# Token attention, mixer and expert layer on one core: folded value-output weight, column-tiled gate and router, eight Gelu buffers, three conv sets

## The chip, the core and the metric

The kernel runs on one core of a Trainium2 chip. The metric is the device time of one execution in microseconds (us); lower is better. A core has a matrix engine (PE, with its weight loads PEld), a vector engine (DVE), a scalar engine for table functions (ACT), a general engine (POOL) and a sync engine (SP) that issues most DMAs. Each runs its own list of instructions in order, and they meet at semaphores only.

## The reference

All arithmetic is fp32. There are 16 images of 96 x 96 and 16 texts of 128 tokens of width 64.

```python
feat = conv2x2_stride2(x) + conv_b                  # 4 channels -> 144 tokens of 64
Q, K, V = feat @ wq.T + bq, feat @ wk.T + bk, feat @ wv.T + bv
tok = softmax(Q @ K.T / 8) @ V @ wo.T + bo
h = concat([tok, txt])                              # 272 tokens for each image
x = layernorm(h)
pos  = running sums of (x@Wvp+bvp) * cos/sin(base_phases), read out, / sqrt(position)
cont = running sums over key phases tanh(tanh(x@Wk1)@Wk2)*pi, read by query phases
gates = softmax(relu(x @ Wg1 + bg1) @ Wg2 + bg2)    # 2 numbers for each token
h = h + (layernorm(gates0*pos + gates1*cont) * ln_g + ln_b) @ Wo + bo
y = layernorm(h)
w = softmax over the two best of y @ Wg + bg        # 8 experts
out = h + sum_e w[e] * (gelu(y @ W1[e] + b1[e]) @ W2[e] + b2[e])   # 64 -> 256 -> 64
```

## The kernel before

Two images form a pair: one lies in partitions 0 to 63, the other in 64 to 127, so there are 8 pairs of 272 columns, 2176 columns in all, or 17 windows of 128 columns. Token attention and the mixer's phases, memory and recall run pair by pair. Layer norms, gate, routing and experts run by 5 groups of windows, `GW = [3, 4, 4, 4, 2]`. A norm needs the features of a token side by side, so a group is transposed by PE before it (h0_t, combine) and back after it (xn_t, norm_s, xn2_t).

The order of work on each engine is written out by hand in `PLAN`: a list of stages with an index for "pe", "dve", "act", "pool" and "sp". Each engine's block loops over its list and issues the instructions of the stage, with the semaphore waits that it needs. `BANKS` names the PSUM bank for each stage and index; `take` in the PE block makes a stage wait until the last reader of its bank is done.

The stages, with their lines:

- **Start.** SP loads the pixels in two halves (`pixa`, `pixb`), weights and text; ACT's queue loads phase, cols, ident, rows (L469 to L472). PE runs ten warm-up matmuls (L865). ACT makes the first tap of the convolution for each half (L478), DVE adds the other three (L618), the first half at once, the second as stages taps:0 to taps:2.
- **Token attention**, by pair: qkv (PE L873 to L877, evicted by DVE L682 and ACT L494, L498), scores (L888), row maximum (DVE L695), Exp with its sums (ACT L504), normalising (DVE L702), transposes (L898) copied by ACT (L514), mix (L909), evicted by ACT with the value bias (L520), tok_out (L915), evicted by ACT into `h0s` (L524).
- **base** (once): DVE reduces the base phases (L671 to L676), ACT takes the sines (L485 to L488), POOL scales them.
- **Mixer**: norm (moments L637 to L649, root on POOL L428, normalise L656), mix_gate (L943: stationary 128 tokens, moving the 32 columns of `g1_w`), gate_z on DVE (L718 to L723: bias, relu times weight difference, sum, bias), Tanh (L538); values (L963) and running sums (L746, L750); hidden and phases (L954, L982), absolute pass on DVE (L756), Sin (L554), memory (L993), mask (L766), recall (L1004, copied by L558); content (L970, L736); combine (L1017, L774 to L778), norm, attn_out (L1030).
- **Routing**, by group: route (L1038: stationary 128 tokens, moving the 16 columns of `gate_w`), the two best of 8 with their one-hots on DVE (L803 to L810), Tanh (L568), weights (L815 to L822), transposed (L1044), written to DRAM and read back broadcast over 64 partitions (`wide`) by SP.
- **Experts**, by group and expert: `expert` (L1070) makes two halves j of the hidden layer, each into two banks by two row tiles; ACT's Gelu (L592) writes one of four buffers `hidden_e`; `expert_out` (L1083) makes the output in two column tiles; DVE adds bias and weights it (L841); POOL adds it up (L463). `finish` (L1055) transposes the sum back, DVE adds it to `res` (L847), SP stores.

ACT's functions come from tables; a change of table shows as ACT_TABLE_LOAD.

## Time and profile before

| | us |
|---|---|
| median of 3 runs | 257.95 |
| all runs | 256.1, 263.72, 257.95 |
| profiled execution: span from first to last instruction | 254.6 |
| PE, DVE, ACT, POOL busy in it | 232.3, 170.6, 158.7, 100.7 |

The profile is of one execution; of its own time the page gives the span. Busy is the time in which an engine has an instruction running; matmuls are pipelined and their ends are modelled, so neighbouring matmuls overlap in it, and starts are the better measure of pace. Windows give busy time by engine in a stretch, with the number of instructions, TensorE's granted clock (1.00 is 2.4 GHz) and the DMA share. Every matmul of the code stands twice in the trace, as two instructions.

### The profile page before, as it was taken

The page shows a single profiled execution, that of the slowest core. Times are in us where ns is not written, and L with a number is a line of the kernel's source. Part 1 is how long each engine was busy: PE and PEld are TensorE (multiplying, and loading weights), DVE is VectorE, ACT ScalarE, POOL GpSimd, SP SyncE. Part 2 cuts the span into 40 slices and gives each one's busy share as a digit, 9 for nine tenths or more (in the row PEclk, how much of TensorE's full clock was granted, in tenths as well). Part 3 has the DMA queues.
Part 4 walks back from the last instruction along what each step waited for, and adds up shares of the span by engine and source line. Part 5 has one row for each costly group of instructions (what it writes and reads, how often), then busy time and mean ns, then how long its engine had stood idle before and what let it go on. Part 6 is the DMA issues. An engine that isn't in the chain of part 4 may idle for free.

```text
span 254.6 us, 4573 instructions
## 1 busy us (share of the span) xinstructions
PE 232.3 (91%) x1511; PEld 128.0 (50%) x1511; DVE 170.6 (67%) x526; ACT 158.7 (62%) x295; POOL 100.7 (40%) x88
## 2 busy tenths in 40 slices
...
GB/s 224 172 225 4 1 3 0 0 3 0 3 3 0 3 0 3 5 173 76 0 0 9 190 140 4 0 0 23 236 111 0 0 28 239 113 0 3 161 48 62
DMA packets 12902, 14.41 MB, mean 57 GB/s; under 512 B 6448, under 2 KB 10576, under 8 KB 12752
## 3 DMA queue, kind: packets, MB, share of 16 engines
...
q8 instruction: 12, 0.20, 0.3%
q14 instruction: 10, 0.08, 0.1%
...
## 4 chain that ended last, share of the span: by engine, by line
PE 61%; DVE 21%; ACT 9%; issue 6%; DMA 1%; POOLq 0%; POOL 0%; DVEq 0%; ACTq 0%
PE ps L1070 24%; PE ps L1083 23%; ACT probs L504 3%; DVE trig L756 2%; DVE stat L637 2%; DVE feat L618 2%; DVE y L746 2%; PE ps L993 2%; PE ps L1030 2%; PE ps L1004 1%; DMA arena<-in_x_a 1%; DVE mem L766 1%; PE ps L1038 1%; DVE negmax L695 1%; PE ps L933 1%
## 5 line engine op out<-in xcount | busy, mean ns | idle before, releaser
L592 ACT ACTIVATE arena<-ps,cols 128x1024 f32<-128x1024 f32 (+2 forms) x80 | 74.0, 984 | 45.9 <-PE ps L1070 34.2
L1070 PE MATMUL ps<-xt,w 64*128 64x512 f32 (+2 forms) x320 | 69.2, 556 | 1.0 <-ACT arena L592 0.4
L1083 PE MATMUL ps<-arena,w 128*64 128x512 f32 (+2 forms) x320 | 64.9, 538 | 0.7 <-ACT arena L592 0.7
L463 POOL TENSOR_TENSOR acc<-acc,scaled 128x512 f32<-128x512 f32 (+2 forms) x35 | 39.6, 1131 | 63.9 <-DVE scaled L841 63.0
L428 POOL TENSOR_TENSOR rstd<-vare,minus_half 128x8 f32<-128x8 f32 (+2 forms) x15 | 25.6, 1710 | 65.0 <-DVE vare L646 65.0
L1070 PEld LDWEIGHTS ps<-xt,w 64*128 64x128 f32 x320 | 29.1, 189 | 32.4 <-issue 23.9
L841 DVE SCALAR_TENSOR_TENSOR scaled<-ps,b_col,wide 128x512 f32<-128x512 f32 (+2 forms) x35 | 23.3, 667 | 31.1 <-PE ps L1083 26.7
L1083 PEld LDWEIGHTS ps<-arena,w 128*64 128x64 f32 x320 | 20.5, 136 | 38.1 <-issue 26.4
L451 POOL TENSOR_TENSOR cum<-cum,turn_n 128x544 f32<-128x544 f32 x8 | 12.1, 1517 | 15.5 <-DVE cum L750 15.5
L504 ACT ACTIVATE probs<-ps,negmax 72x144 f32<-72x144 f32 x32 | 11.6, 375 | 1.3 <-DVE negmax L695 1.3
L618 DVE SCALAR_TENSOR_TENSOR feat<-arena,cols,feat 128x144 f32<-128x144 f32 x24 | 7.1, 362 | 6.6 <-ACT feat L478 6.5
L993 PE MATMUL ps<-trig 64*128 64x272 f32 (+2 forms) x96 | 8.6, 313 | 2.5 <-ACT trig L554 2.0
L750 DVE TENSOR_TENSOR_SCAN cum<-ones,y 128x544 f32<-128x544 f32 x8 | 10.3, 1291 | 0.3
L841 DVE SCALAR_TENSOR_TENSOR acc<-ps,b_col,wide 128x512 f32<-128x512 f32 (+2 forms) x5 | 3.3, 669 | 10.2 <-PE ps L1083 7.7
L544 ACT ACTIVATE hid<-ps,cols 128x544 f32<-128x544 f32 x8 | 5.6, 715 | 7.2 <-PE ps L954 7.2
L993 PEld LDWEIGHTS ps<-trig 64*128 64x128 f32 x96 | 7.5, 186 | 4.7 <-ACT trig L554 2.3
L534 ACT ACTIVATE xt<-ps 128x256 f32<-128x256 f32 (+1 forms) x18 | 5.9, 367 | 5.9 <-PE ps L933 5.6
L766 DVE TENSOR_TENSOR mem<-ps,mask 128x864 f32<-128x864 f32 x8 | 8.3, 1052 | 1.8 <-PE ps L993 1.8
L637 DVE BATCH_NORM_STATS2 stat<-res 128x6 f32<-128x64 f32 x68 | 9.5, 209 | 0.0
L656 DVE TENSOR_TENSOR xn<-xn,rstd 128x512 f32<-128x512 f32 (+2 forms) x10 | 7.5, 751 | 2.6 <-POOL rstd L428 2.6
L865 PE MATMUL ps<-ones 128*128 128x272 f32 x20 | 7.9, 577 | 1.5 <-POOL ones L419 1.5
L789 DVE TENSOR_TENSOR res<-ps,res 128x512 f32<-128x512 f32 (+2 forms) x5 | 3.0, 609 | 8.8 <-PE ps L1030 8.8
...
## 6 DMA issues: line engine op xcount, KB each, us to landing
...
```

The costliest lines, as they stand in the source:

```text
L428: pool.tensor_tensor(rstd[:, kind, g % 2, 0:nb(g)], vare[:, kind, g % 2, 0:nb(g)], minus_half[:, 0:nb(g)], ALU.pow).then_inc(rstd_ok[kind], 1)
L451: link(pool.tensor_tensor(cum[:, i % 2, :, :], cum[:, i % 2, :, :], turn_n[:, :, :], ALU.mult))
L463: pool.tensor_tensor(acc[:, g % 2, 0:128 * GW[g]], acc[:, g % 2, 0:128 * GW[g]], scaled[:, i % 2, 0:128 * GW[g]], ALU.add).then_inc(S["acc ...
L504: ins = act.activation(probs[0:SC, i % 2, k, :], ps[0:SC, bank("scores", i) + k // 2, SI * (k % 2):SI * (k % 2) + SI], ACT.Exp, bias=negma ...
L592: act.activation(hidden_e[:, k % 4, 0:2 * n].rearrange("p (h t) -> p h t", h=2), ps[:, bank("expert", i, j):bank("expert", i, j) + 2, 0:n] ...
L618: dve.scalar_tensor_tensor(out=o, in0=pix[:, v, tap, :].rearrange("p (b s) -> p b s", b=4), scalar=col("conv_w", 4 * c + tap), in1=o, op0= ...
L637: ins = dve.bn_stats(stat[:, g % 2, k, :], src[:, 64 * k:64 * k + 64])
L766: dve.tensor_tensor(mem[:, i % 2, :, :], ps[:, b0:b0 + 2, 0:MEND], over(mask[:, :], 2), ALU.mult)\
L841: dve.scalar_tensor_tensor(out=total, in0=ps[:, bank("expert_out", i), 0:n], scalar=b2_col[:, e:e + 1], in1=wide[:, g % 2, e, 0:n], op0=AL ...
L993: ins = pe.matmul(ps[:, bank("memory", i) + h, MOFF[k]:MOFF[k] + L - q], trig[r, 0, L * i + m:L * i + m + 128], trig[r, 1, L * i + q:L * i ...
L1070: ins = pe.matmul(ps[:, bank("expert", i, j) + h, 0:n], w1[r, c:c + 128], xt[r, GC[g]:GC[g] + n], start=True, stop=True)
L1083: ins = pe.matmul(ps[64 * h:64 * h + 64, bank("expert_out", i), 0:n], w2[:, 2 * (i % E) + j, :], hidden_e[:, (2 * i + j) % 4, n * h:n * h ...
```

## The change

- `wv` and `wo` are multiplied once at the start (transpose, product, and `wo` times `bv`; two copies by ACT), so that mix gives the token output at once: tok_out and its stage on ACT go.
- The gate: `g1_w` is stationary and 128 tokens move, for each window into its own 32 output partitions; ACT evicts with bias and Relu (gate_h), a small matmul sums with the weight difference (gate_z, now on PE), ACT's Tanh reads PSUM. DVE builds the weights for this once (gate_w).
- Routing the same way: `gate_w` is stationary, ACT adds the bias (route_f), a matmul with a part of the identity turns the logits back (logit_t), and DVE's first choice reads PSUM.
- `HIDDEN = 8` Gelu buffers; expert is a stage for each half j with one pair of banks. The arena of the buffers also holds the early tiles.
- Three conv sets of pairs, 0-1, 2-4, 5-7, each with its own loads of pixels; the first taps are stages on ACT.
- `GW = [3, 4, 4, 3, 3]`; moments take two small instructions less; the loads on ACT's queue come as ident, cols, rows, phase; five warm-up matmuls, then one, then one.
- All orders and all banks are written anew.

```diff
-GW = [3, 4, 4, 4, 2]
+GW = [3, 4, 4, 3, 3]
-WARM_UP = 10
+WARM_UP = [5, 1, 1]
+PAIR_SETS = [(0, 2), (2, 5), (5, 8)]
+HIDDEN = 8
...
 "dve"
-taps:0 qkv:0 taps:1 qkv:1 scores:0 scores:1 qkv:2 qkv:3 probs_n:0 probs_n:1 taps:2 scores:2 scores:3 probs_n:2
+base:0 taps:0 taps:1 gate_w:0 taps:2 taps:3 qkv:0 taps:4 qkv:1 taps:5 scores:0 scores:1 qkv:2 taps:6 qkv:3
...
+content:1 content:2 phase_abs:0 phase_abs:1 content:3 content:4 content:5 ln1_stats:4 memory:0 memory:1
+ln1_norm:4 phase_abs:2 phase_abs:3 gate_p:2 combine:0 streams:3 gate_p:3 phase_abs:4 content:6 content:7
+ln2_stats:0 phase_abs:5 memory:2 ln2_norm:0 memory:3 phase_abs:6 phase_abs:7 memory:4 attn_out:0 ln3_stats:0
+memory:5 ln3_norm:0 memory:6 combine:1 memory:7 ln2_stats:1 route:0 ln2_norm:1 route_t:0 streams:4 streams:5
+attn_out:1 ln3_stats:1 streams:6 expert_out:0 ln3_norm:1 expert_out:1 expert_out:2 gate_p:4 expert_out:3
...
 "act"
-qkv:0 qkv:1 exps:0 exps:1 probs_t:0 qkv:2 qkv:3 probs_t:1 exps:2 exps:3 mix:0 mix:1 qkv:4 tok_out:0 tok_out:1
+base:0 tap0:0 tap0:1 tap0:2 fold_t:0 fold:0 qkv:0 qkv:1 exps:0 qkv:2 exps:1 qkv:3 probs_t:0 exps:2 qkv:4 mix:0
...
+mix:6 gate_t:1 h0_t:3 hidden:0 probs_t:7 hidden:1 phases:0 mix:7 phases:1 h0_t:4 hidden:2 phases:2 xn_t:2
+xn_t:3 trig:0 trig:1 hidden:3 phases:3 gate_h:2 gate_h:3 recall:0 recall:1 gate_t:2 trig:2 trig:3 hidden:4
+gate_t:3 xn_t:4 phases:4 hidden:5 gate_h:4 trig:4 phases:5 hidden:6 hidden:7 phases:6 trig:5 phases:7 norm_s:0
+trig:6 trig:7 recall:2 recall:3 recall:4 xn2_t:0 recall:5 route_f:0 expert:0 expert:1 expert:2 recall:6
...
 "pe"
+memory:4 norm_s:0 recall:2 attn_out:0 recall:3 memory:5 recall:4 memory:6 memory:7 combine:1 xn2_t:0 recall:5
+route:0 expert:0 expert:1 expert:2 logit_t:0 recall:6 recall:7 expert_out:0 gate_z:4 values:4 expert:3
...
+expert:56 expert:57 expert:58 expert:59 expert:60 expert:61 expert_out:26 expert_out:27 expert_out:28
+expert_out:29 expert_out:30 finish:2 expert:62 expert:63 expert:64 expert:65 expert:66 expert:67 expert:68
...
 "sp"
-wide:0 wide:1 wide:2 store:0 wide:3 store:1 wide:4 store:2 store:3 store:4
+wide:0 wide:1 store:0 wide:2 store:1 wide:3 wide:4 store:2 store:3 store:4
...
-            act.dma_start(phase[:, :, :], phase_d).then_inc(ld["phase"], 16)
-            act.dma_start(cols[:, :], cols_d).then_inc(ld["cols"], 16)
             act.dma_start(ident[:, :], const_d[:, 0:128]).then_inc(ld["ident"], 16)
+            act.dma_start(cols[:, :], cols_d).then_inc(ld["cols"], 16)
+            act.preload_act_table(ACT.Exp)
             act.dma_start(rows[:, :], rows_d).then_inc(ld["rows"], 16)
+            act.dma_start(phase[:, :, :], phase_d).then_inc(ld["phase"], 16)
...
+            warm_up(WARM_UP[0])
+            pe.wait_ge(ld["tokw"], 16)
+            pe.wait_ge(ld["ident"], 16)
+            pe.transpose(ps[:, FOLD_BANK, 0:128], wv, ident[:, :]).then_inc(S["fold_t"], 1)
+            warm_up(WARM_UP[1])
+            pe.wait_ge(S["wv_t"], 1)
+            pe.wait_ge(ld["cols"], 16)
+            pe.matmul(ps[:, FOLD_BANK, 128:256], wv_t[:, :], wo, start=True, stop=True)
+            pe.matmul(ps[:, FOLD_BANK, 256:257], wo, col("bv"), start=True, stop=True).then_inc(S["fold"], 1)
+            reader[FOLD_BANK] = (S["wvo"], 1)
+            warm_up(WARM_UP[2])
...
-                    pe.wait_ge(S["conv"], 12 if i < 4 else 24)
+                    pe.wait_ge(S["conv"], 12 * (SET_OF[i] + 1))
...
+                    if i == 0:
+                        pe.wait_ge(S["wvo"], 1)
...
-                elif stage == "tok_out":
-                    pe.wait_ge(S["mix_sb"], i + 1)
-                    take(bank("tok_out", i), "h0_sb", i + 1)
-                    pe.matmul(ps[:, bank("tok_out", i), 0:SI], wo, mixed[:, i % 2, :], start=True, stop=True).then_inc(S["tok_mm"], 1)
...
                     for w in range(GW[i]):
                         c = GC[i] + 128 * w
-                        ins = pe.matmul(ps[:, bank("route", i), 16 * w:16 * w + 16], xt[:, c:c + 128], diag(gate_w),
+                        ins = pe.matmul(ps[32 * w:32 * w + 32, bank("route", i), 0:128], gate_w[:, :], xt[:, c:c + 128],
                                         start=True, stop=True)
-                    ins.then_inc(S["lg_mm"], 1)
+                    ins.then_inc(S["lgf_mm"], 1)
+                elif stage == "logit_t":
+                    r = 32 * GW[i]
+                    pe.wait_ge(S["lgf_sb"], i + 1)
+                    take(bank("logit_t", i), "lg_sb", i + 1)
+                    pe.matmul(ps[:, bank("logit_t", i), 0:16 * GW[i]], lg_t[0:r, i % 2, :],
+                              ident[0:r, 0:r].rearrange("p (w q) -> p w q", q=32)[:, :, 0:16], start=True, stop=True)\
+                        .then_inc(S["lg_mm"], 1)
...
+                    act.wait_ge(S["e1_mm"], i + 1)
...
+                    if i >= HIDDEN:
+                        act.wait_ge(S["e2_mm"], (i - HIDDEN) // 2 + 1)
```

## Rows read from the trace of the kernel before

**Rows 1.** Windows of three stretches: length, then busy us (instructions) by engine, clock, DMA, GB/s

```profile
13.90:49.00 35.10, 29.14 (x276) 22.32 (x275) 30.25 (x80) 30.55 (x111) 13.70 (x9) 1.00 0.08 30
49.00:85.70 36.70, 29.68 (x272) 21.24 (x270) 35.59 (x114) 23.58 (x48) 20.55 (x15) 1.00 0.01 1
85.70:249.40 163.70, 161.14 (x913) 75.32 (x912) 95.81 (x306) 98.68 (x125) 63.77 (x53) 0.99 0.26 61
```

**Rows 2.** Timeline of PE at two landmarks: start us, us, engine line, operation, count

```profile
85.69 0.92 PE L1070 MATMUL ps<-xt,w 64*128 64x384 f32 x4
...
249.43 0.66 PE L1055 MATMUL ps<-ident,acc 128*128 128x128 f32 x4
```

**Rows 3.** Timeline of PE in the experts, four windows a group

```profile
206.92 3.70 PE L1070 MATMUL ps<-xt,w 64*128 64x512 f32 x16
210.56 3.65 PE L1083 MATMUL ps<-arena,w 128*64 128x512 f32 x16
214.14 1.99 PE L1070 MATMUL ps<-xt,w 64*128 64x512 f32 x8
216.06 1.94 PE L1083 MATMUL ps<-arena,w 128*64 128x512 f32 x8
```

**Rows 4.** Timeline of PE, routing of a group of four windows

```profile
122.83 0.96 PE L1038 MATMUL ps<-gate_w,xt 128*128 128x16 f32 x8
```

**Rows 5.** Loads of ACT's queue: issue in the timeline, then us to landing (page)

```profile
2.15 0.45 ACTq L472 DMA_DIRECT2D rows<-in_rows  x1
...
phase<-in_phase ACTq DMA_DIRECT2D x1, 272.0 KB, 3.9
rows<-in_rows ACTq DMA_DIRECT2D x1, 97.0 KB, 4.8
```

**Rows 6.** Timeline of DVE and ACT around base: its first instruction, and the next stage's

```profile
24.02 0.29 DVE L671 TENSOR_SCALAR turns<-phase 128x272 f32<-128x272 f32 x1
26.32 0.36 DVE L682 TENSOR_SCALAR qs<-ps,cols 128x144 f32<-128x144 f32 x1
...
26.46 1.28 ACT L485 ACT_TABLE_LOAD   x1
28.97 0.36 ACT L494 ACTIVATE ks<-ps,cols 128x144 f32<-128x144 f32 x1
```

**Rows 7.** Timeline of the start: warm-up matmuls, first taps, other taps, first Exp

```profile
2.11 2.02 PE L865 MATMUL ps<-ones 128*128 128x272 f32 x4
8.28 1.08 PE L865 MATMUL ps<-ones 128*128 128x272 f32 x4
...
5.83 3.29 ACT L478 ACTIVATE feat<-arena,cols 128x144 f32<-128x144 f32 x8
6.47 4.81 DVE L618 SCALAR_TENSOR_TENSOR feat<-arena,cols,feat 128x144 f32<-128x144 f32 x16 [6.47 <-ACT feat L478]
...
13.92 0.38 ACT L504 ACTIVATE probs<-ps,negmax 72x144 f32<-72x144 f32 x1 [0.83 <-DVE negmax L695]
```

**Rows 8.** Groups by line (busy, mean ns | idle), then DVE's timeline: moments, gate, next

```profile
L520 ACT ACTIVATE mixed<-ps,cols 128x144 f32<-128x144 f32 x8 | 3.0, 386 | 1.1 <-PE ps L915 1.1
L756 DVE SCALAR_TENSOR_TENSOR trig<-trig,cols 128x544 f32<-128x544 f32 x8 | 8.2, 1019 | 0.0
L766 DVE TENSOR_TENSOR mem<-ps,mask 128x864 f32<-128x864 f32 x8 | 8.3, 1052 | 1.8 <-PE ps L993 1.8
L736 DVE TENSOR_TENSOR vc<-ps,rows 128x384 f32<-128x384 f32 x8 | 4.4, 548 | 0.0
...
37.08 1.09 DVE L637 BATCH_NORM_STATS2 stat<-res 128x6 f32<-128x64 f32 x8
39.74 0.25 DVE L718 TENSOR_TENSOR gu<-ps,rows 128x96 f32<-128x96 f32 x1
40.74 0.17 DVE L700 RECIPROCAL rinv<-rsum 72x4 f32<-72x4 f32 x1
```

**Rows 9.** Windows: one us in the spell of lower clock (columns as in Rows 1)

```profile
90.00:91.00 1.00, 0.99 (x4) 0.69 (x6) 0.86 (x5) 1.00 (x3) 1.00 (x1) 0.50 0.00 0
```

More of the change, by code:

```diff
@@ L45 @@
 EPS = 1e-5
-WARM_UP = 10
+WARM_UP = [5, 1, 1]
+PAIR_SETS = [(0, 2), (2, 5), (5, 8)]
+SET_OF = [s for s, (a, b) in enumerate(PAIR_SETS) for _ in range(a, b)]
+HIDDEN = 8
 LAST_PAIR = [(GC[g] + 128 * GW[g] - 1) // L for g in range(NG)]
@@ L99 @@
[L99 to L109 removed]
+    "qkv": [(1, 0), (1, 2), (2, 3), (4, 5), (2, 4), (4, 5), (1, 4), (3, 1)],
@@ new lines @@
+    "phases": [(6,), (4,), (2,), (4,), (6,), (6,), (4,), (0,)],
+    "memory": [(0,), (2,), (2,), (6,), (2,), (6,), (4,), (0,)],
+    "recall": [(0,), (1,), (1,), (4,), (0,), (4,), (1,), (6,)],
+    "combine": [(1, 5), (2, 3), (2, 7), (0, 1), (0, 1)],
+    "norm_s": [(0,), (5,), (2,), (0,), (1,)],
+    "attn_out": [(0,), (5,), (2,), (3,), (0,)],
+    "xn2_t": [(6, 7), (1, 4), (1, 2), (1, 2), (4, 5)],
+    "route": [(5,), (1,), (1,), (2,), (3,)],
+    "logit_t": [(0,), (3,), (0,), (0,), (1,)],
+    "weights_t": [(3,), (1,), (3,), (2,), (2,)],
@@ L128 @@
-combine:0 hidden:3 phases:2 content:2 hidden:4 phases:3 mix_gate:2 h0_t:4 content:3 phases:4 norm_s:0 xn_t:3
-memory:2 memory:3 attn_out:0 recall:2 hidden:5 hidden:6 recall:3 values:4 combine:1 phases:5 phases:6 xn2_t:0
-content:4 expert:0 route:0 mix_gate:3 expert:1 expert_out:0 memory:4 norm_s:1 xn_t:4 content:5 values:5
-mix_gate:4 expert:2 attn_out:1 memory:5 hidden:7 recall:4 recall:5 expert_out:1 weights_t:0 expert:3 combine:2
-content:6 expert_out:2 expert:4 expert_out:3 phases:7 memory:6 expert:5 expert_out:4 expert_out:5 xn2_t:1
@@ L133 @@
-norm_s:2 expert:6 attn_out:2 route:1 recall:6 expert_out:6 expert:7 expert:8 expert_out:7 expert:9 content:7
-values:6 expert_out:8 weights_t:1 memory:7 expert:10 recall:7 values:7 xn2_t:2 expert:11 expert_out:9
-expert_out:10 expert_out:11 expert:12 expert:13 expert_out:12 combine:3 expert_out:13 expert:14 expert:15
-expert:16 expert_out:14 expert_out:15 route:2 expert:17 expert_out:16 norm_s:3 finish:0 weights_t:2 expert:18
-attn_out:3 combine:4 expert_out:17 expert:19 expert_out:18 expert_out:19 expert:20 expert:21 expert:22
@@ new lines @@
+phases:3 mix_gate:2 mix_gate:3 recall:0 recall:1 gate_z:2 xn_t:4 gate_z:3 combine:0 hidden:4 values:3 phases:4
+hidden:5 mix_gate:4 content:6 content:7 phases:5 hidden:6 hidden:7 memory:2 phases:6 phases:7 memory:3
+memory:4 norm_s:0 recall:2 attn_out:0 recall:3 memory:5 recall:4 memory:6 memory:7 combine:1 xn2_t:0 recall:5
+route:0 expert:0 expert:1 expert:2 logit_t:0 recall:6 recall:7 expert_out:0 gate_z:4 values:4 expert:3
+expert:4 norm_s:1 values:5 weights_t:0 expert_out:1 attn_out:1 expert:5 expert:6 values:6 expert:7 expert:8
```

427 lines of the change are left out of this document (230 added, 197 removed), and 4 rows, old and new, of the table BANKS.

## The prediction

> **What bounds the kernel now.** I read the windows first, cut at four landmarks: the first Exp at 13.9 us, the last copy of transposed probabilities (done at 49.0), the first expert matmul (85.7) and the end of the last expert output (249.4, where the finishing transposes follow) [rows 1, 2]. From 13.9 to 49.0 (stage A, token attention) three engines are loaded alike: ACT is busy 30.55 of 35.1 us (87%), DVE 30.25, PE 29.14. From 49.0 to 85.7 (stage B, mixer) DVE is the bound, 35.59 of 36.7 us (97%), ACT at 23.58. From 85.7 to 249.4 (stage C, experts) PE is the bound, 161.14 of 163.7 us; DVE and ACT have over 60 us to spare. So an edit pays in C only if it takes work from PE, in B only from DVE, in A from all three. Ahead of A lie 13.9 us of start, behind C a tail of 254.6 - 249.4 = 5.2 us.
>
> A busy PE can be a slow PE, so next I read its timeline in C. From one run's start to the next, 16 expert matmuls take 3.64 us, 8 take 1.92, and 16 output matmuls 3.58 [rows 3]. Eight more cost 1.72, 0.215 each; over that a run pays 0.20 (expert) or 0.14 (output), 0.17 in the mean: the price of changing kinds.
>
> **The change, stage by stage.** *Stage C.* The expert matmuls stay: 17 windows x 8 experts x 2 layers x 8 instructions, each a quarter of 0.215 us, are 117.0 us. Counted in PE's orders, runs of expert and expert_out fall from 56 to 39, since eight Gelu buffers let PE go further ahead: 17 x 0.17 = 2.9 us less. If the 0.17 belongs to something else than the change of kind, nothing is gained; with 0.20 for every run, 3.4. Of the smaller stages, summed by start-to-start times read as in [rows 3], the old order leaves 31.3 us behind the first expert and the new one 19.5: 10.6 have moved ahead of it (memory, recall, content, phases of the later pairs), the rest is routing. Four windows of routing took 0.96 us [rows 4]. In four column tiles they stream 128 columns each, and no row has four tiles at once: the bounds are 0.25 us for a group (all overlap) and 0.96 (none does). I take 0.3, because two tiles overlap in [rows 3] (0.215 us for 512 columns, where the untiled warm-up needs a quarter of 1.08 for 272 [rows 7]), and 0.25 for the added transposing matmul. No overlap would cost 2.4 us here, and as much for the gate in B. The Trainium skill, page TensorEngine Tiling, section Theoretical Speedup, allows up to 4x where a dimension is at most 32; no run here shows it, and the sum by it would be the same.
>
> Before: 117.0 + 56 x 0.17 + 31.3 - 0.75 (transposes behind 249.4) = 157.1 of the measured 163.7; 6.6 us are waits and a spell of half clock. After: 117.0 + 39 x 0.17 + 19.5 - 0.75 = 142.4, and 4.5 for waits (bounds 1 and 9): 146.9 us. The edits of DVE and ACT in this stage (the routing bias as an ACT copy, some small DVE instructions less) count nothing: PE's 161 us cover them. One wait is new: DVE's expert_out:0 waits for the first broadcast load, and ln3_norm:1, so xn2_t:1, now stands behind it. PE has eleven expert tiles, four outputs and smaller stages to do by then, some 20 us, about the length of that chain. SP's order only moves one store ahead of a load. The tail's last group has three windows for two: 0.6 more, 5.8.
>
> *Start.* DVE and ACT now begin with base:0, and ACT's first convolution tap (tap0) is queued behind it. base needs the phase load, which moves from first to last of four on ACT's DMA queue. The last was issued at 2.15 and took 4.8 us [rows 5]: phase lands near 7.0. With its own 3.9 it would be 6.0; the other way I allow the same 1 us. Then DVE reduces for 2.3 us, and ACT loads a table and makes the sines in 2.5 [rows 6]: tap0 starts near 11.8, where it started at 5.83 [rows 7]. The smaller pixel loads hide under this. From tap0 to the first Exp were 8.1 us. Changes there: gate weights on DVE between the taps, ten small instructions, +2.4; a first conv set of half the columns, 12 taps at about 0.22 us for 0.30 [rows 7], -1.0; the Exp table, which now has to be loaded again, +1.28; and PE. PE has idled for ten us by then, waiting for a folded weight that ACT copies behind all twelve tap0 instructions. The kernel's first matmuls took 2.02 us for four, later ones 1.08 [rows 7]; two projections at half speed, +1.7. First Exp at 11.8 + 8.1 + 4.4 = 24.3 instead of 13.92.
>
> *Stage A.* ACT's 30.55 us lose one eviction of 0.386 for seven pairs (2.7), the sines with their table (2.5), the reload of Exp's (1.3) and one pair's phases (1.0), and gain gate and transposed copies (1.8): 24.9 us [rows 6, 8]. At 87% busy that is 28.6 us, at 80% 31.1; DVE has the last taps to do here, so I take 30. Stage A ends at 54.3, 5.3 later than before.
>
> *Stage B.* DVE's 35.6 us change by three more absolute passes (+3.1), two more memory masks (+2.1), four more content adds (+2.2), one more normalise (+0.5), two gate sums of about 1.1 gone to PE and ACT (-2.2), one set of moments earlier (-2.7), four cheaper sets (two of the seven small steps gone, -1.1) and combine:1 later (-1.3) [rows 8]: 36.2. ACT rises from 23.6 to about 34: its table loads here go from five to nine (Sin and Tanh alternate), and the phases and sines of the last three pairs come in. PE comes to about 34 too. So B turns from a stage with one bound into one like A. At A's 87% it takes 41.6 us, at its own 97% 37.3, at 80% 45. I take 41.6, as the loads are those of A. First expert at 95.9, 10.2 later than 85.69 [rows 2].
>
> **The sum.** 95.9 + 146.9 + 5.8 = 248.6 us of span for 254.6. The three runs of before lie 1.5, 3.35 and 9.1 us above the profiled span; between the first two I take 2.4 and predict 251 us, 2.7% under the median of 257.95.
>
> **The rivals.** *The start costs nothing in the end*: phase early, A and B packed as B was. First expert at 88, span 88 + 146.9 + 5.8 = 240.7, time 243. For it speaks that DVE was kept 97% busy for 36.7 us; against it, that two other engines had slack then. 0.2.
> *B packs worse than A*, at 80% or less, since each pair goes through phases, absolute, sine, memory, mask and recall on three engines with nine table loads between; or the column tiles don't overlap. First expert at 100 to 103, span 253 to 256, time 255 to 258: no change. 0.2.
> *PE stays at half clock through A.* In the old trace the clock fell to 0.50 (1.2 GHz) near 89.6, after PE had been kept waiting, for some 3 us [rows 9]; now PE idles from about 6 to 16 us. A holds about 29 us of PE work; at half clock PE becomes its bound, and each us of that work done so adds nearly one. Past 14 us of it beyond what I count, the whole is slower than 263; with half of A's work, 15 more, 266. Against it: A ran at 1.00 with PE 83% busy [rows 1]. 0.1. The Trainium skill, page TensorE: Matmul & The Clock Gate, section HAM oscillation, has waits between bursts put the array back to half clock each time; the trace agrees in that one spell.
> *What I forecast*, 246 to 256: 0.5.
>
> **How the numbers follow.** About 2% is what a measurement of this kernel can tell from no change: 252.8 to 263.1. Of the forecast's half, 0.3 lies below 252.8 and 0.2 above; with the first rival faster has 0.5, with the second the same has 0.4, slower 0.1. The range, 242 to 260, leaves out half of the first rival and the third.
>
> **What would show it.** Right: tap0 near 12 us behind a table load; PE idle from 6 to 16; first Exp at 24; last copy of probabilities near 54; nine table loads from there to the first expert at 96; then 16 matmuls still in 3.6 us, 39 runs in 147 us, and four windows of routing in 0.3. Wrong: tap0 before 9, B over in 37 us or taking 46, or PE kept waiting in C for more than 9.

## The result, and the profile after

The changed kernel takes 264.75 us (median of four executions, 262.87 to 267.14; the four of before beside them 256.1 to 263.72). The ratio is 1.024, 95% interval 1.014 to 1.034: slower, where 251 and a gain had been forecast; whether by more than 2% the interval leaves open. Its profiled execution has a span of 262.4 us, 7.8 more than before. Executions of one kernel differ here by how long PE had half clock: the 91 executions of before that stand beside the runs below reach from a mean granted clock of 0.998 (span 254.3) to 0.951 (262.6), so a ratio compares only executions within 1.5% of the fastest of their kernel, while a median holds them all.

Windows of the changed kernel, cut at the same landmarks as [rows 1, 2]: up to the first Exp, stage A, stage B, stage C, tail (length, busy us and instructions of PE, PEld, DVE, ACT, POOL, granted clock, DMA share, GB/s).

```profile
0.00:21.41 21.41, 12.19 (x58) 10.07 (x59) 12.20 (x43) 11.30 (x26) 2.83 (x12) 0.76 0.64 185
21.41:61.38 39.97, 36.23 (x282) 27.48 (x282) 31.72 (x99) 27.72 (x106) 13.75 (x10) 0.79 0.00 1
61.38:108.54 47.16, 38.06 (x369) 27.52 (x367) 39.63 (x84) 36.04 (x62) 20.48 (x16) 0.93 0.00 1
108.54:256.58 148.04, 145.04 (x807) 66.43 (x804) 88.30 (x264) 83.72 (x112) 61.20 (x50) 1.00 0.27 67
256.58:262.40 5.82, 1.10 (x8) 0.62 (x6) 1.64 (x3) 0.00 (x0) 1.52 (x2) 0.89 0.31 68
```

Against before: start +7.5 us, A +4.9, B +10.5, C -15.7, tail +0.6. Against the forecast: first Exp -2.9, A +10.0, B +5.6, C +1.1, tail 0: the 13.8 us between 248.6 and 262.4. The expert stage came as forecast; what it gave was lost ahead of it, and the clock column says where to look first: 0.79 in stage A, where it had been 1.00. (The 0.76 ahead of A is a stretch of half clock from 8 to 19 us, behind the long wait at the start.)

Windows of the same kernel inside stage A.

```profile
36.00:38.00 2.00, 1.91 (x24) 1.35 (x20) 1.76 (x6) 1.06 (x5) 1.43 (x1) 1.00 0.00 0
38.00:40.00 2.00, 0.99 (x6) 0.34 (x3) 1.85 (x4) 1.89 (x9) 1.18 (x3) 1.00 0.03 8
40.00:42.00 2.00, 1.20 (x15) 0.81 (x15) 1.93 (x13) 1.95 (x11) 1.29 (x1) 1.00 0.00 0
42.00:44.00 2.00, 1.78 (x12) 1.58 (x14) 1.93 (x6) 1.45 (x6) 1.70 (x1) 0.67 0.00 0
44.00:46.00 2.00, 2.00 (x10) 1.25 (x7) 1.05 (x2) 1.60 (x8) 1.13 (x2) 0.50 0.00 0
...
50.00:52.00 2.00, 2.00 (x14) 1.60 (x13) 2.00 (x4) 0.22 (x1) 1.53 (x2) 0.50 0.00 0
...
56.00:58.00 2.00, 2.00 (x8) 1.86 (x9) 0.34 (x3) 0.50 (x2) 0.75 (x1) 0.50 0.00 0
58.00:60.00 2.00, 2.00 (x9) 0.96 (x7) 1.52 (x2) 0.49 (x1) 0.00 (x0) 0.56 0.00 0
60.00:62.00 2.00, 2.00 (x20) 1.28 (x22) 1.97 (x10) 1.36 (x3) 1.34 (x1) 1.00 0.00 0
```

From 38 to 42 PE has nearly half its time free; after that the clock is 0.50 (1.2 GHz) for some 17 us. Such a change is called a fall below, and the stretch at 0.50 a spell. In the spell PE is busy in every us; ACT stands much of the time, DVE only in part of it. PE's timeline shows the long wait of the start, the four short ones ahead of the fall, one group at half clock, a wait in stage B behind which no fall came (the clock was 1.00 from 91 us on), and the pace of the experts.

```profile
14.13 0.80 PE L936 MATMUL ps<-tokw,wv_t 128*128 128x128 f32 x2 [7.73 <-ACT wv_t L527]
...
38.73 0.44 PE L1003 MATMUL ps<-ident,xn 128*128 128x128 f32 x2 [0.51 <-DVE xn L724]
39.67 0.33 PE L1003 MATMUL ps<-ident,xn 128*128 128x128 f32 x1 [0.50 <-ACT res L574]
40.48 0.69 PE L972 MATMUL ps<-ident,arena 72*72 72x72 f32 x8 [0.48 <-DVE arena L772]
...
42.22 1.21 PE L1046 MATMUL ps<-vc_w,xt 128*128 128x128 f32 x6 [0.54 <-ACT b_col L636]
...
55.85 1.65 PE L1046 MATMUL ps<-vc_w,xt 128*128 128x128 f32 x6
...
98.83 0.52 PE L1099 MATMUL ps<-ident,comb 128*128 128x128 f32 x3 [2.83 <-ACT trig L604]
...
131.04 0.43 PE L1114 MATMUL ps<-xt,gate_w 128*32 128x128 f32 x8
131.40 1.56 PE L1152 MATMUL ps<-xt,w 64*128 64x384 f32 x8
...
206.12 3.65 PE L1165 MATMUL ps<-arena,w 128*64 128x512 f32 x16
209.70 5.21 PE L1152 MATMUL ps<-xt,w 64*128 64x512 f32 x28
```

Sixteen output matmuls still take 3.58 us from start to start, as in [rows 3]; four windows of routing take 0.36 where they took 0.96 [rows 4]. ACT's timeline at the start:

```profile
2.91 1.28 ACT L535 ACT_TABLE_LOAD   x1
8.32 0.43 ACT L535 ACTIVATE turn_p<-phase 128x272 f32<-128x272 f32 x1 [4.12 <-DVE phase L744]
...
9.53 4.39 ACT L523 ACTIVATE arena<-arena,cols 128x72 f32<-128x72 f32 x12
...
20.11 1.28 ACT L554 ACT_TABLE_LOAD   x1
21.41 0.38 ACT L554 ACTIVATE arena<-ps,negmax 72x144 f32<-72x144 f32 x1
```

The Sin table is loaded at 2.91, while ACT still waits for the reduced phases; tap0 starts at 9.53 (5.83 before [rows 7]).

### The profile page after: what moved, and what is told of

Its sections match the earlier page's. It is cut to its first block, busy times and chain, and to the rows that moved or that the text cites. A ratio compares the mean times of both kernels' runs of the same rounds, so it can differ in the third digit from the quotient of the medians.

```text
span 262.4 us, 4560 instructions
## 1 busy us (share of the span) xinstructions
PE 232.6 (89%) x1514; PEld 132.1 (50%) x1514; DVE 173.5 (66%) x490; ACT 158.8 (61%) x304; POOL 99.8 (38%) x88
## 4 chain that ended last, share of the span: by engine, by line
PE 56%; DVE 20%; ACT 11%; issue 7%; POOL 2%; DMA 1%; POOLq 0%; ACTq 0%; DVEq 0%
PE ps L1165 17%; PE ps L1152 16%; DVE stat L704 2%; PE ps L1069 2%; PE ps L983 2%; PE ps L1080 2%; DVE y L804 2%; ACT arena L523 2%; PE ps L1046 2%; PE ps L972 1%; ACT L609 1%; DVE xn L724 1%; DMA phase<-in_phase 1%; POOL rstd L469 1%; PE ps L1093 1%
## 5 line engine op out<-in xcount | busy, mean ns | idle before, releaser
L654 ACT ACTIVATE arena<-ps,cols 128x768 f32<-128x768 f32 (+1 forms) x80 | 73.1, 991 | 33.8 <-PE ps L1152 31.7
L1152 PE MATMUL ps<-xt,w 64*128 64x384 f32 (+1 forms) x320 | 65.4, 542 | 0.0
L504 POOL TENSOR_TENSOR acc<-acc,scaled 128x384 f32<-128x384 f32 (+1 forms) x35 | 38.8, 1109 | 66.8 <-DVE scaled L900 65.8
L1165 PE MATMUL ps<-arena,w 128*64 128x384 f32 (+1 forms) x320 | 61.9, 533 | 0.0
L900 DVE SCALAR_TENSOR_TENSOR scaled<-ps,b_col,wide 128x384 f32<-128x384 f32 (+1 forms) x35 | 23.2, 668 | 48.1 <-PE ps L1165 47.6
L469 POOL TENSOR_TENSOR rstd<-vare,minus_half 128x6 f32<-128x6 f32 (+1 forms) x15 | 26.3, 1752 | 60.2 <-DVE vare L713 60.2
L580 ACT ACTIVATE xt<-ps 128x256 f32<-128x256 f32 (+1 forms) x20 | 6.3, 351 | 10.6 <-PE ps L1003 10.3
L554 ACT ACTIVATE arena<-ps,negmax 72x144 f32<-72x144 f32 x32 | 11.6, 373 | 1.5 <-DVE negmax L765 1.5
L724 DVE SCALAR_TENSOR_TENSOR xn<-xn,rstd 128x384 f32<-128x384 f32 (+1 forms) x10 | 10.1, 1019 | 2.0 <-POOL rstd L469 2.0
L678 DVE SCALAR_TENSOR_TENSOR arena<-arena,cols 128x108 f32<-128x108 f32 (+1 forms) x36 | 9.5, 330 | 1.8 <-ACT arena L523 1.8
L1046 PE MATMUL ps<-vc_w,xt 128*128 128x128 f32 x48 | 9.5, 365 | 0.5 <-ACT b_col L636 0.5
```

Source lines behind the costliest of these rows:

```text
L469: pool.tensor_tensor(rstd[:, kind, g % 2, 0:nb(g)], vare[:, kind, g % 2, 0:nb(g)], minus_half[:, 0:nb(g)], ALU.pow).then_inc(rstd_ok[kind], 1)
L504: pool.tensor_tensor(acc[:, g % 2, 0:128 * GW[g]], acc[:, g % 2, 0:128 * GW[g]], scaled[:, i % 2, 0:128 * GW[g]], ALU.add).then_inc(S["acc ...
L554: ins = act.activation(probs[0:SC, i % 2, k, :], ps[0:SC, bank("scores", i) + k // 2, SI * (k % 2):SI * (k % 2) + SI], ACT.Exp, bias=negma ...
L654: act.activation(hidden_e[:, i % HIDDEN, 0:2 * n].rearrange("p (h t) -> p h t", h=2), ps[:, b:b + 2, 0:n], ACT.Gelu, bias=col("b1", 2 * e ...
L724: return dve.scalar_tensor_tensor(out=blocks(dst[:, 0:64 * n]), in0=blocks(dst[:, 0:64 * n]), scalar=8.0, in1=spread(rstd[:, kind, g % 2, ...
L900: dve.scalar_tensor_tensor(out=total, in0=ps[:, bank("expert_out", i), 0:n], scalar=b2_col[:, e:e + 1], in1=wide[:, g % 2, e, 0:n], op0=AL ...
```

## The experiments

Theory after the result: the order of the change is worth what was forecast, and half clock ahead of the experts takes it back. Rival: the order itself makes the start, A and B longer, and the clock follows. Each run stands with its ratio to before (95% interval); "first expert" is the start of expert:0, which closes stage B. The stages are those of the one profiled execution, whose own time stands in the column "profiled"; where it differs from the median, the other executions had another clock. Stage C took 148.0 to 148.2 us in every one but e8_pool_light (146.4), so everything is decided ahead of it.

| kernel | first Exp | A | B | first expert | profiled us | median us | ratio |
|---|---|---|---|---|---|---|---|
| before | 13.92 | 35.1 | 36.6 | 85.7 | 256.1 | 258.6 to 261.1 | 1 |
| after | 21.41 | 40.0 | 47.2 | 108.5 | 264.15 | 264.75 | 1.024 [1.014, 1.034] |
| e1_fill_mid | 21.82 | 35.0 | 48.9 | 105.8 | 262.22 | 261.5 | 1.012 [1.006, 1.018] |
| e5_fill_all | 19.81 | 35.1 | 49.5 | 104.4 | 260.07 | 260.28 | 1.008 [1.005, 1.011] |
| e6_trig_together | 22.29 | 40.0 | 45.2 | 107.4 | 262.97 | 264.31 | 1.021 [1.008, 1.034] |
| e7_all_mended | 15.11 | 38.4 | 48.4 | 102.0 | 257.54 | 260.24 | 1.004 [0.999, 1.010] |
| e9_best | 13.29 | 44.5 | 45.1 | 102.8 | 258.44 | 261.41 | 1.010 [1.003, 1.017] |
| e12_base_at_start | 15.13 | 39.1 | 45.5 | 99.8 | 255.44 | 258.12 | 0.996 [0.991, 1.001] |
| e13_gate_w_early | 16.03 | 35.9 | 45.6 | 97.6 | 253.15 | 253.07 | 0.982 [0.977, 0.987] |
| e14_group0_first | 15.26 | 36.3 | 51.1 | 102.7 | 258.27 | 261.42 | 1.012 [1.007, 1.017] |

**Unread matmuls where PE waited before the fall.** Several runs use such a fill: ahead of a stage, n matmuls of `ones` into a bank whose last reader is done and that a later stage overwrites. `FILL` gives for each stage the bank, n and the columns.

```diff
+FILL = {'xn_t:0': (3, 3, 128), 'probs_t:4': (3, 2, 128), 'bias_t:0': (3, 2, 128)}
...
+            def fill(b, n, cols):
+                if b in reader:
+                    pe.wait_ge(*reader[b])
+                for _ in range(n):
+                    pe.matmul(ps[:, b, 0:cols], ones[:, 0:128], ones[:, 0:cols], start=True, stop=True)
             for stage, i in PLAN["pe"]:
+                if f"{stage}:{i}" in FILL:
+                    fill(*FILL[f"{stage}:{i}"])
```

> The changed kernel with seven unread 128-column matmuls on PE ahead of xn_t:0, probs_t:4 and bias_t:0, where PE waited four times about 0.5 us between 38.2 and 42.8 us before its granted clock fell from 1.00 to 0.50. They write a bank that nothing else holds. Theory (the fall in stage A is what costs stage A its 10 us, and the waits ahead of it bring it about): the clock stays at 1.00 through 42 to 60, the last probs_t copy of the stage ends at 51 to 55 instead of 61.4, the first expert starts 7 to 10 us earlier than at 108.5, the time is 255 to 258. Rival (the order of the work in stage A sets its length and the clock only follows): the clock stays at 1.00 but the stage still ends within 3 us of 61.4, the time is 262 to 265. Third case (a fill of 1.5 us is too little or the fall has another cause): the clock falls all the same within 42 to 46 and the time does not move.

Windows of e1_fill_mid: stage A, and stage B in two parts.

```profile
21.82:56.84 35.02, 30.57 (x296) 23.36 (x296) 29.84 (x92) 27.55 (x106) 13.94 (x9) 1.00 0.01 1
56.84:79.00 22.16, 18.50 (x161) 13.20 (x159) 21.89 (x46) 15.92 (x29) 15.98 (x12) 0.85 0.01 2
79.00:105.78 26.78, 21.57 (x208) 15.97 (x209) 18.40 (x46) 20.36 (x34) 5.24 (x4) 0.87 0.00 1
```

The fall of stage A is gone with seven small matmuls, so the waits ahead of it brought it about. But A fell to 35.0, not to 30: the spell of 17 us cost 5 us. By the prediction's rival, where each us of PE's work done at half clock adds nearly one, its 8.5 us of work would have added some 8. Not all of the 5 came through: DVE did 92 instructions in the shorter stage where it had done 99, and the other seven in B (48 for 41 up to hidden:4's Tanh). The median fell by 3.3, since other spells (0.85 and 0.87 in B) came besides.

**The start.** Between fold transpose and fold product PE got 14 more warm-ups.

```diff
-WARM_UP = [5, 1, 1]
+WARM_UP = [5, 15, 1]
```

> The changed kernel with 14 more warm-up matmuls between the transpose of the value weights and the fold product, where PE stands from 6.4 to 14.1 us. Theory (the half-speed projections at 16 to 18.8 are a cost of the start): the granted clock is 1.00 from 10 to 20, the first Exp starts at 19.5 to 20.5 instead of 21.4, the time falls by 1 us. Rival (DVE's taps set the first Exp and PE's pace there is hidden): the first Exp stays at 21.2 to 21.5 and the time stays within 1 us. Either way the fall at 42 should stay, since the waits at 38 to 42 are the same.

First Exp 19.90, the 1.5 us of half-speed projections, as the theory had it; with an unchanged start it came between 21.20 and 22.29 (e4, e6), so the 1.5 is uncertain by half a us. The fall of stage A came all the same, but for some 10 us only (0.61 in the windows from 40 to 44 and 48 to 52, 0.50 between them), and A took 36.9 us. The time says nothing: four executions from 260.97 (clock 0.960, the profiled one) to 270.84 (0.918). Then the sines were put behind the first taps:

```diff
 "dve"
-base:0 taps:0 taps:1 gate_w:0 taps:2 taps:3 ...
+taps:0 taps:1 taps:2 base:0 gate_w:0 taps:3 ...
 "act"
-base:0 tap0:0 tap0:1 tap0:2 fold_t:0 fold:0 qkv:0 ...
+tap0:0 tap0:1 tap0:2 fold_t:0 fold:0 base:0 qkv:0 ...
```

> The changed kernel with base:0 moved behind the first set of taps on DVE and behind the taps and the fold on ACT, where ACT has little to do between 14 and 19 us. Theory (tap0 waits for nothing but the sines): tap0 starts at 6.5 to 7 instead of 9.5, the first Exp at 18 to 19 instead of 21.4, the time falls by 2 to 3 us. Rival (the 2.3 us of reduction and 1.2 us of sines only change places, DVE or ACT is as late at the first Exp): first Exp at 20.5 to 22, the time within 1 us. With another phase of the start the fall of the clock in stage A may come elsewhere or not at all: if it goes, the time falls by 7 to 10 more.

First Exp at 17.30, 4.1 us earlier, more than expected, and the median 260.76 (1.004, interval 0.998 to 1.010). The start's slip is real and comes through. Its profiled execution had two falls of the clock in A and is longer than its median (span 266.7), so its stages are not used.

**Stage B's two falls.** In FILL: `'memory:0': (4, 3, 272), 'phases:4': (1, 4, 272)`.

> The changed kernel with unread matmuls on PE in the two waits of stage B after which the granted clock fell: three of 272 columns ahead of memory:0 (wait of 1.7 us from 71.2) and four ahead of phases:4 (wait of 2.8 us from 82.4). Theory (the falls at 73.7 to 76.6 and 87.0 to 90.5 follow those waits and lengthen the stage by half of their 6.4 us): both falls go, stage B takes 44 to 45 us instead of 47.1, the time is 2 to 3 lower. Rival (from 80 on ACT's alternation of tables sets the stage, PE's slower pace is hidden): the falls go and stage B stays within 1 us of 47.1. The fall at 42 stays.

Neither of the two falls came; stage B took 47.6 us from 66.96 to 114.56, after's 47.2. That is the rival's number, but not for its reason. Up to hidden:4's Tanh (pair 4 of 0 to 7) B took 21.4 us where it had taken 23.0: the first spell had cost 1.5. Behind that, phases:4 followed that Tanh 0.4 us later than in the changed kernel, being behind a fill, and another fall came at 103, behind a wait of 2.83 us. What the second spell costs stays open.

This execution also had two spells in A, some 31 us together (time 270.12, median 268.46), and so prices them: e1, e2, the changed kernel and e4 have the same orders in A, and the stage took 35.0, 36.9, 40.0 and 45.8 us with none, some 10, 17 and 31 us at half clock.

**All the waits at once.** The 14 warm-ups as above, and fills ahead of mix:0, xn_t:0, probs_t:4, bias_t:0, phases:2, xn_t:2, xn_t:3, memory:0, phases:4 (5) and norm_s:0 (5).

> The changed kernel with unread matmuls on PE in all the longer waits ahead of the experts: the 14 warm-ups of the start, and two to five ahead of mix:0, xn_t:0, probs_t:4, bias_t:0, phases:2, xn_t:2, xn_t:3, memory:0, phases:4 and norm_s:0. Some 12 us of PE work more, nearly all of it in waits. Theory (the order of the change is worth what was forecast and PE's half clock ahead of the experts takes it back): the clock is 0.98 or more, the first expert starts at 98 to 101 instead of 108.5, stage C is 148.0 as in every kernel so far, the time is 253 to 257, faster than before by 1.5 to 3 %. Rival (the order itself is the loss): the clock is as high, but the first expert starts at 105 or later and the time is 261 or more.

Windows of e5_fill_all: A, and B in two parts.

```profile
19.81:54.90 35.09, 31.27 (x302) 24.06 (x302) 29.90 (x92) 27.61 (x106) 13.94 (x9) 1.00 0.01 2
54.90:78.00 23.10, 21.39 (x182) 14.44 (x181) 22.82 (x47) 17.12 (x31) 16.01 (x12) 1.00 0.01 2
78.00:104.36 26.36, 24.60 (x227) 18.82 (x225) 17.49 (x45) 19.07 (x33) 5.25 (x4) 0.94 0.00 1
```

At a clock of 0.989 the time is still 260.28, and the theory falls in its first form: with the clock back, A is 35.1 and B 49.5. With these fills the order is 3.7 us longer than before (span 258.3). The first half of B is DVE's (22.82 of 23.10 us). In the second half one spell of 3.4 us was left, and fills stood in PE's way: phases:4 and norm_s:0 each followed ACT's step ahead of them about 1 us later than in the changed kernel. So the 3.7 us are not the order's alone.

**Table loads.** ACT's order alone:

```diff
-... gate_h:4 trig:4 phases:5 hidden:6 hidden:7 phases:6 trig:5 phases:7 norm_s:0 trig:6 trig:7 recall:2 ...
+... gate_h:4 phases:5 hidden:6 hidden:7 phases:6 phases:7 trig:4 trig:5 trig:6 trig:7 norm_s:0 recall:2 ...
```

> The changed kernel with ACT's order alone altered between 86 and 101 us: phases:5 to phases:7 first, then trig:4 to trig:7 together, then norm_s:0. Four of the nine table loads of that stretch go, 1.28 us each. Theory (ACT's alternation of tables sets the end of stage B): the first expert starts 3 to 5 us earlier after trig:4's place, the time falls by 3 to 5. Rival (the loads lie in waits of ACT, or norm_s:0 behind trig:7 holds up attn_out:0 and the experts): the first expert moves by less than 1.5 us either way. The falls of the clock at the start and in stage A are untouched by this, though their places can differ between executions.

Five table loads instead of nine between trig:0 and the experts, 5.1 us of ACT gone; B became 2.0 us shorter and the time 264.31. But most of the 2.0 lies ahead of the place where the orders differ. Up to hidden:4's Tanh the two kernels are alike, and only the changed one had a spell there; the 24 instructions of memory:0 and memory:1 show it (windows and PE's timeline, the changed kernel, then e6_trig_together):

```profile
61.38:84.34 22.96, 17.70 (x161) 12.06 (x159) 22.30 (x41) 17.13 (x30) 15.24 (x12) 0.93 0.01 2
72.94 3.41 PE L1069 MATMUL ps<-trig 64*128 64x272 f32 x24 [1.71 <-DVE vc L794]
...
62.26:83.58 21.32, 16.24 (x161) 10.85 (x159) 21.05 (x41) 17.04 (x30) 14.88 (x12) 1.00 0.01 2
73.46 2.03 PE L1069 MATMUL ps<-trig 64*128 64x272 f32 x24 [1.61 <-DVE vc L794]
```

So 1.6 us are the absent spell of 3.4 us. From there to the first expert, with one spell of 3.4 us in each, it is 23.8 us for 24.2: the new order gave 0.4. PE now waits for the batch instead:

```profile
96.27 1.10 PE L1069 MATMUL ps<-trig 64*128 64x272 f32 x12 [2.41 <-ACT trig L609]
```

Fewer loads in this order are worth 0.4 us, not 3 to 5; what loads cost that nothing waits for instead, no run shows. Then the first sum of remedies: taps ahead of base:0, gate_w:0 ahead of ln1_stats:0, fold steps between the taps, `preload_act_table(ACT.Sin)`, the trig order, the fills of e5 and six more ahead of scores:0, with two warm-ups added instead of 14.

> The changed kernel with the start put back (base:0 behind the first taps, gate_w:0 in DVE's waits at 30 us, the value fold between the taps, the Sin table loaded first), the trig steps together as in the run of that alone, and unread matmuls on PE in its waits. If all three causes are real and add up: first Exp at 14 to 16 instead of 21.4 (minus 6), stage A 31 to 33 us instead of 40 (minus 8), stage B 38 to 41 instead of 47.1 (minus 7), so the first expert at 85 to 90, stage C 148.0 and the time 241 to 247, faster than before by 5 to 8 %. If they share one cause (only the clock, say), the time is that of the run with unread matmuls alone, 253 to 257.

The clock was 0.999 and the start 6.3 us earlier, but A took 38.4 and B 48.4: neither of the two numbers that the theory had for full clock. PE stood 2.96 us, to 17.69, for the second conv set's taps (no fall followed), and fills ahead of phases:4 and norm_s:0 now stood in PE's way: from phases:4 on B took 23.4 us, and 21.5 in e12_base_at_start below, which has fewer fills there.

**What holds stage B at full clock.** POOL's residual sums and position products were narrowed in e5's kernel (that part of the output is left out; it narrows POOL's work in stage C too).

```diff
-pool.tensor_tensor(res[:, cut(i)], res[:, cut(i)], xn[:, i % 2, 0:128 * GW[i]], ALU.add)
+pool.tensor_tensor(res[:, cut(i)][:, 0:64], res[:, cut(i)][:, 0:64], xn[:, i % 2, 0:64], ALU.add)
...
-link(pool.tensor_tensor(cum[:, i % 2, :, :], cum[:, i % 2, :, :], turn_n[:, :, :], ALU.mult))
+link(pool.tensor_tensor(cum[:, i % 2, :, 0:32], cum[:, i % 2, :, 0:32], turn_n[:, :, 0:32], ALU.mult))
```

> The kernel of e5_fill_all with POOL's residual additions cut to 64 columns and its position products to 32, so those parts of the output are left out; every wait and every instruction of the other engines stays. It tells what bounds stage B at full clock. Theory (DVE is the bound of the first 23 us of stage B, 99 % busy, and POOL slows it): phase_abs falls from 1.42 us on average to about 0.78 (four of them, 2.6 us), the normalisation from 0.97 to 0.56 (three, 1.2 us), the stage up to the first hidden tile of pair 4 shrinks by 3 to 4 us and the first expert starts 3 to 4 us before 104.4. Rival (the chain of ACT, PE and DVE from 78 us on sets the first expert and DVE's gain is waited away): DVE's instructions get as much shorter but the first expert moves by less than 1 us.

DVE's groups in the first half of stage B (busy us, mean ns), e5_fill_all from 54.9 to 78:

```profile
L815 DVE SCALAR_TENSOR_TENSOR trig<-trig,cols 128x544 f32<-128x544 f32 x4 | 5.5, 1421 | 0.0
L725 DVE SCALAR_TENSOR_TENSOR xn<-xn,rstd 128x384 f32<-128x384 f32 (+1 forms) x3 | 2.8, 969 | 0.0
```

and e8_pool_light from 52.99 to 75:

```profile
L815 DVE SCALAR_TENSOR_TENSOR trig<-trig,cols 128x544 f32<-128x544 f32 x4 | 3.1, 815 | 0.0
L725 DVE SCALAR_TENSOR_TENSOR xn<-xn,rstd 128x384 f32<-128x384 f32 (+1 forms) x3 | 1.8, 632 | 0.0
```

The instructions became nearly as short as expected and the first expert came at 101.16, 3.2 us earlier. Of that, 1.7 us are stage A's (33.4 for 35.1) and 2.0 stage B's (47.5 for 49.5); the start was 0.4 later. All of B's 2.0 came ahead of phases:4, where DVE's busy time fell from 24.3 to 19.2 us and PE, with its fills, was then busy 22.6 of 23.0. So DVE bounds there, and POOL's work beside it lengthens DVE's. The Trainium skill, page SBUF — State Buffer, section Who interferes with whom, says that a DVE instruction with two SBUF inputs contends with a GpSimd instruction that reads SBUF; the absolute pass has two, and the trace agrees.

**The order mended, with and without fills.** As e7, but base:0 in stage A (ACT ahead of exps:4, DVE with gate_w:0 ahead of ln1_stats:0), fewer fills (none ahead of norm_s:0); and the same order with none at all.

> The changed kernel with the sine tables of the base moved on into stage A, as the kernel before has them (base:0 and gate_w:0 on DVE ahead of ln1_stats:0, base:0 on ACT ahead of exps:4, on POOL behind ln1_stats:0), the fold between the first taps, the trig steps together and unread matmuls in PE's waits, fewer than in e7_all_mended where they were in the way (none ahead of norm_s:0, two instead of five ahead of phases:4, three ahead of memory:4). Against e7_all_mended: first Exp at 12 to 13 instead of 15.1, the third pair's projections at 14 instead of 17.7, no 2.4 us of filling behind the last wait. First expert at 95 to 97 instead of 102, stage C 148.0, time 250 to 253, faster than before by 2.5 to 4 %. If stage A is as late because ACT now carries two more table loads and 1.3 us of sines there, the first expert is at 99 to 101 and the time 254 to 257.

> The same order as e9_best with no matmul added, neither at the start nor later. Theory (the clock costs PE's work where PE is the bound, most of it in stage A): the granted clock falls for 15 to 25 us ahead of the experts, the first expert is 4 to 8 us later than in e9_best, the time 255 to 261. Rival (what the added matmuls win in clock they cost in PE's order): within 1 us of e9_best.

e9_best: first Exp 13.29, near the 12 to 13 expected, but A 44.5 us. PE was busy 1.48 of 4 us from 32 to 36, and the clock was 0.50 or little more from 35 to 52. e10_best_nofill: 264.02, ratio 1.006 (0.9997 to 1.011), first expert 104.63. Its windows show the same more strongly:

```profile
28.00:32.00 4.00, 2.66 (x28) 1.80 (x28) 3.79 (x20) 3.48 (x7) 1.06 (x1) 1.00 0.00 0
32.00:36.00 4.00, 1.17 (x3) 0.47 (x3) 3.59 (x6) 3.68 (x12) 3.33 (x4) 0.59 0.01 4
36.00:40.00 4.00, 3.39 (x21) 2.64 (x21) 3.86 (x19) 3.59 (x18) 2.92 (x2) 0.50 0.00 0
40.00:44.00 4.00, 4.00 (x23) 3.09 (x23) 1.59 (x3) 1.34 (x8) 2.52 (x2) 0.50 0.00 0
```

So in the profiled executions fills won 1.8 us up to the first expert at this order, not 4 to 8, and the ratios don't tell the two kernels apart. Two ways out of the wait were tried: base:0 earlier on DVE and gate_w:0 behind ln1_norm:0 (with two more fills), or the sines at the start and gate_w:0 likewise behind ln1_norm:0.

> The order of e9_best with base:0 on DVE put into its wait ahead of probs_n:3 and gate_w:0 behind ln1_norm:0, and two more unread matmuls ahead of scores:6. In e9_best PE stood 1.55 and 1.04 us between 32 and 36 us behind DVE's base:0 and gate_w:0, and the clock then stayed at 0.50 from 35 to 52. Theory (that wait is what starts the fall, and the fall is what held e9_best): the clock is 0.98 or more, the first expert starts at 95 to 98 instead of 102.8, the time 250 to 253. Rival (the two table loads and three sines that ACT carries in stage A are the loss): the first expert at 100 to 103 with or without a fall, the time 255 to 261.

> The order of e7_all_mended (sines ahead of the first Exp, from a table that is loaded before anything is due) with taps:3 ahead of base:0, gate_w:0 behind ln1_norm:0 and no unread matmuls where PE was the bound (none ahead of norm_s:0, two instead of five ahead of phases:4). Theory (in e7_all_mended the wait of 3 us for the second set's taps and some 4 us of needless filling are the rest of the loss): the third pair's projections start at 15.5 to 16.5 instead of 17.7, the first expert at 96 to 98 instead of 102, the time 251 to 254, faster than before by 2 to 4 %. Rival (DVE sets stage A and the first half of stage B however the start is arranged): the first expert at 100 to 102, the time 255 to 259.

e11_base_in_a: 261.83 (1.005, 0.999 to 1.011); PE stood 2.90 us at 37.05 for ACT, and the clock was down from 38 to 59. e12_base_at_start: 258.12, not told apart from before, and again one wait and one fall. Its PE timeline and windows:

```profile
42.16 1.18 PE L981 MATMUL ps<-ident,arena 72*72 72x72 f32 x8 [1.83 <-DVE arena L773]
```

```profile
40.00:42.00 2.00, 0.32 (x2) 0.00 (x0) 1.97 (x4) 0.73 (x5) 1.96 (x1) 0.98 0.00 0
42.00:44.00 2.00, 1.84 (x12) 1.63 (x12) 1.96 (x4) 1.87 (x10) 1.13 (x2) 0.50 0.00 0
44.00:48.00 4.00, 4.00 (x30) 2.68 (x30) 3.96 (x4) 1.37 (x5) 3.92 (x3) 0.50 0.00 0
```

**That wait taken away, by one move.**

```diff
 "dve"
-... qkv:6 ln1_stats:0 scores:4 qkv:7 ln1_norm:0 scores:5 probs_n:4 gate_w:0 ln1_stats:1 ...
+... qkv:6 gate_w:0 ln1_stats:0 scores:4 qkv:7 ln1_norm:0 scores:5 probs_n:4 ln1_stats:1 ...
```

> The kernel of e12_base_at_start with gate_w:0 on DVE ahead of ln1_stats:0 (where e7_all_mended had it) instead of behind ln1_norm:0. In e12_base_at_start PE stood 1.83 us from 40.3 behind DVE, and the clock was 0.50 from 42 to 49. Theory (a wait of PE of 1.5 us or more in stage A brings a fall; without it there is none): the clock is 0.99 or more, the last probs_t copy ends by 52 instead of 54.2, the first expert starts at 97.5 to 98.5 instead of 99.75, the time is 1 to 2 below that of e12_base_at_start. Rival: the clock is higher, the first expert within 0.5 us of 99.75, since DVE sets it.

```profile
40.00:42.00 2.00, 1.77 (x16) 1.37 (x16) 1.70 (x3) 1.68 (x8) 1.26 (x1) 1.00 0.00 0
42.00:44.00 2.00, 1.94 (x27) 1.35 (x28) 1.97 (x3) 1.30 (x5) 1.92 (x2) 1.00 0.00 0
...
16.03:51.96 35.93, 32.03 (x308) 24.94 (x308) 32.06 (x101) 27.61 (x106) 14.89 (x10) 1.00 0.10 39
51.96:97.55 45.59, 42.31 (x398) 30.08 (x396) 40.22 (x91) 30.73 (x58) 21.70 (x16) 1.00 0.01 1
```

No fall in any of four executions (clocks 0.995 to 0.998), 252.87 to 253.25 us: 5 us below e12_base_at_start's median, more than the 1 to 2 expected, since most of that kernel's executions had a lower clock (0.970) than its profiled one (0.986; 255.44 us, 2.3 above this kernel's). This beats both kernels: 0.982 of before (0.977 to 0.987; whether by more than 2% stays open) and 11.7 us below the changed one's median. Last, stage B was reordered (group 0 first, content:3 to content:5 and phase_abs:2 and :3 behind combine:0, trig:2 and trig:3 into the batch, memory:2 on behind norm_s:0):

> The kernel of e13_gate_w_early with the order of stage B altered: combine:0, ln2 and the steps of group 0 come as soon as pairs 0 and 1 have been recalled, content:3 to content:5 and phase_abs:2 and phase_abs:3 after them, trig:2 and trig:3 with the other trig steps (two table loads fewer). Nothing is added. It tells whether stage B is long because of the order in which ACT and DVE are served there: PE then has content:3 to content:5 in its wait ahead of phases:4, DVE has 4.5 us less ahead of combine:0, ACT 2.56 us less ahead of hidden:4. Theory: stage B 42 to 44 us instead of 46, first expert 3 to 4 us earlier than in e13_gate_w_early, time 250 to 252, faster than before by 2 to 4 %. Rival (the sum of DVE's and ACT's work ahead of the first expert sets it whatever the order): first expert within 1 us of e13_gate_w_early.

It went the other way: B 51.1 us. PE now stood in new places, the longest behind DVE's running sums of pair 3:

```profile
79.03 0.42 PE L1017 MATMUL ps<-xt,g_w 128*32 128x128 f32 x6 [2.77 <-DVE y L800]
```

Order does move B by five us, but not this order; whether one exists that makes B 42 at this load stays open.

## Why the prediction was wrong

- **Stage C, right.** 148.0 for 146.9, tail 5.8 for 5.8; 39 runs, routing 0.36 for 0.3. Over the summed 142.4 there are 5.6 us where 4.5 were allowed; PE stood for 148.04 - 145.04 = 3.0 of them. Prices read as starts of neighbouring runs [rows 3] carried over; no run changes the number of runs alone, so the 0.17 us for each is not shown by itself.
- **Start, right in kind.** First Exp 21.4 for 24.3. Phase landed at 5.88, not 7.0, and the Sin table was loaded ahead of the wait, not behind it; tap0 at 9.5 for 11.8. The half-speed projections (1.7 allowed) were about 1.5 by e2_fill_start.
- **Stage A, the step that failed.** "24.9 us at 87%, I take 30", that is 83%: ACT had 27.7 us, and at full clock the stage takes 35.0 to 35.1 (e1, e5), ACT then 79% busy. So 2.8 us of work were missing from the sum, and a share of busy time read from one order did not carry over to another: the waits there end with DVE and ACT in turn, which is read from the timelines and tested by no run. That is 5 us. The other 5 are the half clock, which stood among the rivals at 0.1.
- **The rival of half clock: mechanism right, price and place wrong.** It was to start with the idle start and cost 15 us. The spell of the start ended at 19 us, ahead of A. Another started with four waits of 0.5 us in the middle of A, and 17 us of it cost 5; at full clock PE waits for DVE and ACT in part of that time. How long it lasts is chance: e4's execution, with the same orders in A, had some 31 us and lost 10.7. "A ran at 1.00 with PE 83% busy" was a mean over a stage, and the new order has its waits of PE close together, from 38 to 42.
- **Stage B, mis-sized.** 47.2 for 41.6, and 49.5 with fills at 1.00 and 0.94 (e5). DVE's work was 39.6 us for 36.2: three more memory masks, not two (+1.1), and instructions that took longer beside POOL than priced (a normalise of three windows 0.94 us, 0.53 before); without most of POOL's work B is 2.0 us shorter (e8). "At A's 87%" was 84%. The spell in the first half of B cost 1.5 to 1.6 us (e4, e6), and the second's price is open. The nine table loads were there as counted; five in their place changed B by 0.4 (e6). At full clock, with that order and fills, B takes 45.6 (e13): some 4 us over the forecast are not the clock's.
- **The sum.** A gain of 15.7 in C stands against 7.5 at the start, 10.5 in B and 4.9 in A. The start's part was a matter of order alone (4.1 us back in e3, 6.3 in e7). Stage B's fits the 10.6 us of work that moved ahead of the experts, where DVE sets the pace, out of C, where PE did; no run moved it back, so that is argued. The chance of 0.1 for slower was too low: two of the three stages were costed by a share of busy time.
